# Causal self-attention on f16 high and low parts instead of f32, with the query and key rows turned tile by tile inside the attention's block

## The reference

```
x = x + cross_attention(layernorm(x), context)   # 16 heads, fake-quantised to 8 bits
x = x + self_attention(layernorm(x))             # the part that is changed
x = x + ffn(layernorm(x))                        # FP4 weights, 2816 hidden, RMS norm of the result

# self_attention, B=4 batches, S=128 tokens, H=16 heads of D=64:
q, k, v = x@Wq + bq, x@Wk + bk, x@Wv + bv        # rope on q and k
scores = einsum('bshd,bthd->bhst', q, k) / sqrt(64), -inf above the diagonal
out = einsum('bhst,bthd->bshd', softmax(scores), v) @ Wo + bo
```

## Time and profile before

| | us |
|---|---|
| median of the runs | 2849.79 |
| the profiled execution | 2849.09 |
| its span, first to last instruction | 2847.3 |
| TensorE busy in the span | 2580.7 |
| VectorE busy | 1833.1 |
| ScalarE busy | 1041.4 |
| GpSimd busy | 554.3 |
| mean granted TensorE clock | 0.969 of full speed |

### The profile page before, as it was taken

How to read it: one execution, slowest core, us unless ns; L and a number is a source line. 1 busy time by engine, 2 the same in 40 slices (tenths; PEclk the granted TensorE clock), 3 DMA queues, 4 the chain that set the end, 5 groups by cost and what they waited for, 6 DMA issues and landing times. The chain is left out here.

```text
span 2847.3 us, 42128 instructions
## 1 busy us (share of the span) xinstructions
PE 2580.7 (91%) x16680; PEld 1315.8 (46%) x16680; DVE 1833.1 (64%) x2736; ACT 1041.4 (37%) x929; POOL 554.3 (19%) x206
## 2 busy tenths in 40 slices
PE   6999999999999999999967777777777999999998
PEld 3444444444444444444434444444444448544443
DVE  5855555555555555555488999999983434667673
ACT  3111111111111111111278999999992215311100
POOL 0500000000000000000055664654631280100100
PEclk9999999999999999999999999999998995899999
DMA  6233443443344344334377889788865214000000
GB/s 244 59 101 99 118 103 87 112 110 89 95 125 109 75 110 119 93 91 118 93 183 185 187 199 207 182 197 206 187 134 209 89 60 76 1 16 1 15 4 30
DMA packets 557198, 321.52 MB, mean 113 GB/s; under 512 B 401953, under 2 KB 533281, under 8 KB 552353
## 3 DMA queue, kind: packets, MB, share of 16 engines
q1 hardware_dynamic: 557088, 319.91, 44.2%
HBM read 149.95 MB, written 69.21 MB: 77 GB/s over the span
## 5 line engine op out<-in xcount | busy, mean ns | idle before, releaser
L502 PE MATMUL kv_acc<-kv_whi,kv_xthi 128*128 128x512 f16 x2048 | 777.4, 380 | 5.3 <-DVE kv_xtlo L558 5.3
L502 PE MATMUL kv_acc<-kv_wlo,kv_xthi 128*128 128x512 f16 x2048 | 777.4, 380 | 0.0
L502 PE MATMUL kv_acc<-kv_whi,kv_xtlo 128*128 128x512 f16 x2048 | 777.2, 379 | 0.0
L957 DVE TENSOR_SCALAR_CACHE_REDUCE at_sc<-at_score 128x1024 f32<-128x1024 f32 x512 | 609.7, 1220 | 26.0 <-PE at_score L838 21.6
L1055 ACT ACTIVATE at_sc<-at_sc,at_bias,at_qs 128x4096 uint16<-128x4096 f32 x128 | 484.8, 3791 | 0.9 <-DVE at_bias L969 0.9
L545 ACT ACTIVATE kv_parts<-kv_key 128x1024 f16<-128x1024 f32 x64 | 67.6, 1057 | 863.5 <-DVE kv_key L583 863.5
L502 PEld LDWEIGHTS kv_acc<-kv_whi,kv_xthi 128*128 128x128 f16 x2048 | 200.6, 98 | 247.9 <-DVE kv_xtlo L558 5.8
L502 PEld LDWEIGHTS kv_acc<-kv_whi,kv_xtlo 128*128 128x128 f16 x2048 | 200.7, 98 | 242.4 <-issue 1.4
L502 PEld LDWEIGHTS kv_acc<-kv_wlo,kv_xthi 128*128 128x128 f16 x2048 | 200.6, 98 | 241.9 <-issue 1.1
L564 DVE SCALAR_TENSOR_TENSOR kv_key<-kv_acc,kv_bias 128x512 f32<-128x512 f32 x128 | 88.5, 691 | 339.7 <-PE kv_acc L502 339.7
L853 PE MATMUL at_turn<-ident,at_sc 128*128 128x128 f16 x2048 | 150.4, 223 | 122.2 <-DVE at_probt L975 91.8
(11 more groups left out here) (203 smaller groups left out, 3125.8 us busy)
## 6 DMA issues: line engine op xcount, KB each, us to landing
kv_rows<-in_ctx SPq DMA_DIRECT2D x64, 512.0 KB, 7.9
keys_turned<-kv_kt SPq DMA_DIRECT2D x32, 1024.0 KB, 5.2
values<-kv_val SPq DMA_DIRECT2D x32, 1024.0 KB, 9.5
at_v_raw<-values SPq DMA_DIRECT2D x16, 2048.0 KB, 8.7
at_kt<-keys_turned SPq DMA_DIRECT2D x32, 512.0 KB, 5.2
x<-keys_turned SPq DMA_DIRECT2D x31, 512.0 KB, 5.1
wq_stage<-in_wkv SPq DMA_DIRECT2D x4, 2048.0 KB, 7.5
x<-in_x SPq DMA_DIRECT2D x2, 2048.0 KB, 8.2
```

The source lines that it names most:

```text
L502: last = nc.tensor.matmul(acc[c][:], a[s][:, k, :], b[:, c, k, :], start=(k == 0 and q == 0), stop=(k == KD - 1 and q == 2))
L957: nc.vector.tensor_scalar(sc[n % 2][:, c * SC:(c + 1) * SC], score[pos % 2][:], 1.0, None, ALU.mult, ALU.max, accum_out=part_max[n % 2][:, ...
```

## The change

- q, k, v and the probabilities are kept as f16 high and low parts, scaled by 16 (q, k, v) and by 1024 (probabilities: ln 1024 is added to the negated maximum by one more small VectorE instruction). Scores and sums are three f16 products in place of one f32 product; four transposes of f32 probabilities become eight of f16.
- The turning block is gone. Its turns are units of one matrix (16 of them: tile, half, q or k), `turn_rows`, four transposes each, three ahead of the loop, one behind `scores(0)` and then one per group up to group 11. ScalarE makes the high part (`high_rows`), VectorE the low part (`low_rows`).
- GpSimd splits the probabilities of each group, between `exps` and `turns`, and before its first group the second half of v in four tiles of three instructions. The first half of v is split at the end of the projection before by ScalarE and VectorE (`values_high`, `values_low`).
- The turned probabilities are copied out by ScalarE in even groups and by VectorE in odd ones, as 16-bit words.
- The bias rows of q, k and v serve as buffers; the feed-forward loads wait until all 16 units are turned.
- Panel 9 is split in the output projection, behind the fourth unit of o, and the products, takes and normalisations go in a new ORDER: (0,0), (1,0), (0,1), (1,1), (2,0), ...
- The wait of `exps` for the reciprocals and the order of TensorE's queue in the loop are as they were.

```diff
@@ attend_causal, sync
             sp.dma_start(*row).then_inc(feed.row_loaded, 16)
+            sp.wait_ge(y_turned, len(units))
             feed.load(sp, 0)
@@ tensor
+            def turn_rows(n):
+                t, h, q = units[n]
+                if n >= 2:
+                    pe.wait_ge(lo_ready, n - 1)
+                for k in range(4):
+                    at = (4 * h + k) * P
+                    last = nc.tensor.transpose(y_bank[n % 2][:, k, :], (y_q, y_k)[q][:, t, at:at + P], ident32[:])
+                last.then_inc(y_turned, 1)
+
             def scores(g):
...
+                pe.wait_ge(lo_ready, 4 * t + 2 * (c // 2) + 2)
...
+                    for n, (a, b) in enumerate(((0, 0), (0, 1), (1, 0))):
+                        last = nc.tensor.matmul(score[g % 2][:, j, :], q_parts[a][rows, at, tok], k_parts[b][rows, at, tok],
+                                                start=(n == 0), stop=(n == 2))
             def turns(g):
-                pe.wait_ge(exps_done, HG * (g + 1))
+                pe.wait_ge(p_split, g + 1)
                 if g >= 2:
-                    pe.wait_ge(p_out, g - 1)
-                for j in range(HG):
-                    last = nc.tensor.transpose(turn[g % 2][:, j, :], s[g % 2][:, j, :], ident32[:])
+                    pe.wait_ge(p_out[g % 2], g // 2)
+                for n in range(2 * HG):
+                    last = nc.tensor.transpose(turn[g % 2][:, n, :], p_parts[g % 2][:, n, :], ident16[:])
                 last.then_inc(p_turned, 1)
...
+            for n in range(3):
+                turn_rows(n)
             scores(0)
+            turn_rows(3)
             for g in range(G):
                 if g + 1 < G:
                     scores(g + 1)
+                if g + 4 < len(units):
+                    turn_rows(g + 4)
                 turns(g)
                 if g >= 1:
                     sums(g - 1)
@@ vector
             for g in range(G):
-                if g == G // 2:
-                    panels.low(dve, split)
                 if g + 1 < G:
                     masks(g + 1)
+                if g + 4 < len(units):
+                    low_rows(g + 4)
+                if g % 2:
+                    turned_out(g)
                 if g >= 1:
                     outputs(g - 1)
@@ scalar
             for g in range(G):
+                if g + 4 < len(units):
+                    high_rows(g + 4)
                 if g + 1 < G:
                     exps(g + 1)
-                turned_out(g)
-                if g == G // 4:
-                    panels.high(act, split)
+                if g % 2 == 0:
+                    turned_out(g)
+        @block.gpsimd
+        def _(pool):
+            def split_values(t):
+                half = slice(HALF, D)
+                nc.gpsimd.tensor_scalar(y_v[:, t, half], y_v[:, t, half], PART, None, ALU.mult).then_inc(v_step, 1)
+                pool.wait_ge(v_step, 2 * t + 1)
+                nc.gpsimd.tensor_copy(v_parts[0][:, t, half], y_v[:, t, half]).then_inc(v_step, 1)
+                pool.wait_ge(v_step, 2 * t + 2)
+                nc.gpsimd.tensor_tensor(v_parts[1][:, t, half], y_v[:, t, half], v_parts[0][:, t, half], ALU.subtract)\
+                    .then_inc(v_split, 1)
+            def split_probabilities(g):
+                pool.wait_ge(exps_done, HG * (g + 1))
+                if g >= 2:
+                    pool.wait_ge(p_turned, g - 1)
+                hi, lo = p_parts[g % 2][:, 0:HG, :], p_parts[g % 2][:, HG:2 * HG, :]
+                nc.gpsimd.tensor_copy(hi, s[g % 2]).then_inc(p_hi_ready, 1)
+                pool.wait_ge(p_hi_ready, g + 1)
+                nc.gpsimd.tensor_tensor(lo, s[g % 2], hi, ALU.subtract).then_inc(p_split, 1)
+            for t in range(T):
+                split_values(t)
+            for g in range(G):
+                split_probabilities(g)
@@ project_and_feed_forward, vector
             for n in range(len(units)):
                 low_o(n)
+                if n == 3:
+                    panels.low(dve, first + 1)
             make(0)
             dve.wait_ge(row_added, 1)
-            for t in range(T):
-                take_x(t, 0)
-                take_x(t, 1)
-                normalise(t)
-                if t:
+            for t, n in ORDER:
+                take_x(t, n)
+                if n == 1:
+                    normalise(t)
+                if n == 1 and t:
                     low_x(2 * t - 2)
                     low_x(2 * t - 1)
```

More of the change, by code:

```diff
@@ L262, in project @@
 def project(chip, tag, panels, first, count, split_first, split_after, rows, addend, out, added=None, beside=None,
-            stats=None):
+            stats=None, after=None):
     nc = chip.nc
@@ L288, in _ @@
                 panels.high(act, m)
+            if after is not None:
+                after[1](act)
         @block.vector
@@ L308, in _ @@
                     panels.low(dve, m)
+                if after is not None and n == after[0]:
+                    after[2](dve)
             dve.wait_ge(panels.taken, T * (first + count))
@@ L1100, in rotate, with attend_causal @@
     return n + 4 * T
-def attend_causal(chip, y_q, y_k, y_v, mask, o, ident32, q_t, panels, split, feed, row):
+def attend_causal(chip, y_q, y_k, y_v, mask, o, ident32, ident16, q_parts, v_parts, spare, feed, row):
     nc = chip.nc
-    turned, q_out, k_out = chip.sem("ca_turned"), chip.sem("ca_q_out"), chip.sem("ca_k_out")
-    scored, masked, maxed = chip.sem("ca_scored"), chip.sem("ca_masked"), chip.sem("ca_maxed")
-    exps_done, p_turned, p_out = chip.sem("ca_exp"), chip.sem("ca_p_turned"), chip.sem("ca_p_out")
+    y_turned, hi_ready, lo_ready = (chip.sem(f"ca_{n}") for n in ("turned", "hi", "lo"))
+    v_step, v_split, p_hi_ready, p_split = (chip.sem(f"ca_{n}") for n in ("v_steps", "v_split", "p_hi", "p_split"))
+    scored, masked = chip.sem("ca_scored"), chip.sem("ca_masked")
+    max_found, maxed = chip.sem("ca_max_found"), chip.sem("ca_maxed")
+    exps_done, p_turned = chip.sem("ca_exp"), chip.sem("ca_p_turned")
+    p_out = [chip.sem("ca_p_out_scalar"), chip.sem("ca_p_out_vector")]
     summed, inv_ready, o_ready = chip.sem("ca_summed"), chip.sem("ca_inv"), chip.sem("ca_o")
     HG = 4
+    PART, LN_PROB = X_SCALE, float(np.log(1024.0))
     groups = [(t, c) for t in range(T) for c in range(HEADS // HG)]
     G = len(groups)
+    units = [(t, h, q) for t in range(T) for h in range(2) for q in range(2)]
     def head_of(c, j):
@@ L1123, in attend_causal, with part @@
         inv = [chip.sb(ctx, f"ca_inv{j}", [P, HG], F32) for j in range(2)]
[L1124 to L1155 removed]
+        y_bank = [chip.ps(ctx, f"ca_y{n}", [P, 4, P], F32) for n in range(2)]
         score = [chip.ps(ctx, f"ca_score{n}", [P, HG, P], F32) for n in range(2)]
[L1158 removed]
+        turn = [chip.ps(ctx, f"ca_turn{n}", [P, 2 * HG, P], F16) for n in range(2)]
         outp = [chip.ps(ctx, f"ca_outp{n}", [P, HG, P], F32) for n in range(2)]
         block = ctx.enter_context(nc.Block())
+        def part(n, e):
+            t, h, q = units[n]
+            return parts[q][e][:, 4 * h:4 * h + 4, t * P:(t + 1) * P]
         @block.sync
@@ L1245, in _, with high_rows @@
         def _(act):
+            def high_rows(n):
+                act.wait_ge(y_turned, n + 1)
+                nc.scalar.activation(part(n, 0), y_bank[n % 2][:], ACT.Copy, scale=PART).then_inc(hi_ready, 1)
             def exps(g):
@@ L1385, in project_and_feed_forward, with done @@
     units = [(t, h) for t in range(T) for h in range(2)]
+    ORDER = [(0, 0), (1, 0), (0, 1), (1, 1)] + [(t, n) for t in range(2, T) for n in range(2)]
+    def done(t, n):
+        return ORDER.index((t, n)) + 1
     with ExitStack() as ctx:
@@ L1449, in products @@
             def products(t, n):
+                pe.wait_ge(panels.lo_ready, first + n + 1)
                 pe.wait_ge(o_lo_ready, 2 * t + 2)
                 if t >= 2:
-                    pe.wait_ge(wo_taken, 2 * (t - 2) + n + 1)
+                    pe.wait_ge(wo_taken, done(t - 2, n))
                 w_hi, w_lo = panels.parts[first + n]
@@ L1474, in _ @@
                 turn_o(n)
-            pe.wait_ge(panels.lo_ready, first + 2)
-            for t in range(T):
-                for n in range(2):
-                    products(t, n)
-                if t:
+            for t, n in ORDER:
+                products(t, n)
+                if n == 1 and t:
                     turn_x(2 * t - 2)
@@ L1641, in _ @@
                 high_o(n)
+                if n == 3:
+                    panels.high(act, first + 1)
             act.wait_ge(feed.raw_loaded, 16 * GROUPS)
```

119 lines of the change are left out of this document (64 added, 55 removed).

## The result

| | before | after |
|---|---|---|
| median of the runs, us | 2849.53 | 2869.55 |
| spread of the runs | 2849.25 to 2851.23 | 2868.89 to 2870.11 |
| the profiled execution, and its span | 2849.09, 2847.3 | 2869.78, 2868.0 |
| busy: TensorE, VectorE | 2580.7, 1833.1 | 2564.4, 1867.8 |
| busy: ScalarE, GpSimd | 1041.4, 554.3 | 1046.8, 596.7 |

The ratio is 1.0069, with a 95% interval of 1.0051 to 1.0086: the change makes the kernel 20 us slower. 2866.1 was forecast, with 2853 to 2877 as range.

The account below looks back on a forecast made before the run. It took a serial chain through ScalarE, TensorE and VectorE, closed by the reciprocal, to bound the attention loop, with GpSimd put into it. +9.2 (attention) and +7.1 (projection) gave +16.3 us: 2866.1 us, range 2853 to 2877.

Parts of the forecast that it names:

- The chain that the prediction rests on: Attention loop: exponentials, GpSimd's split, turns, sums, reciprocal, next exponentials follow serially; anything between exponentials and turns is paid in full.
- The loop: Attention groups: 5.69 us each against 4.73, +0.96; sums give back 1.10, turns cost 0.10 more, GpSimd 1.96.
- The start: Before the loop: GpSimd's value splits take 11.4 us; exponentials of group 2 at about 2364.1, against 2365.37 before.
- the scaling of a value tile on GpSimd: In `split_values` at the start: 0.80 us for each of four tiles, taken between 0.61 and 1.15.
- The end of the loop: Last exponentials to the next stage's first transpose: 7.56 us against 7.3; the stage begins 9.2 us later.
- The projection: Output projection: normalised rows at 30.7, TensorE idle 4.4 us, clock dip 2.7; +7.1 us, bounds 4.4 and 8.5.
- The moved feed-forward loads: Loads moved behind the last row turn, about 2417: all there by about 2451, costing nothing, with 5 us of cover.
- The hidden value steps: VectorE behind panel 8: four steps of about 0.7 us cost nothing under 4.49 us idle; without cover 2.8.
- The tiny addition in `masks`: VectorE in the attention loop: held by a GpSimd split at most 1.15 us, staying inside the slack.
- B: Rival, chance 0.14: f16 keeps the clock up at 2.4 GHz, 5.0 us a group; +4.4, so 2854 us.
- D: Rival, chance 0.10: clock up as in B and GpSimd's copy costs 0.24; 4.6 us a group, 2845 us.
- C: Rival, chance 0.12: GpSimd's one-input steps cost as much as the subtraction; +28.5, so 2878 us.

Follow-up runs that it names:

- filler: Kernel after plus eight unread f16 products of 256 columns in each group, between the turned rows and the turns of the probabilities: 2864.9 us, ratio 1.0054.
- c1: Kernel after with a third buffer of row totals, panel 9 made in group 0 of the attention and the projection's old ORDER: 2839.6 us, ratio 0.9965.
- late filler: Kernel after with third buffer, value splits behind groups 1, 5 and 9, and eight unread f16 products in each of groups 12 to 15: 2845.2 us.

## Why the prediction was right, and where it wasn't

The forecast's sum was +16.3 us and the profiled execution shows +20.7. Of the 4.4 between them, 1.8 lies ahead of the changed code and isn't the change's, 1.7 is the first turning, 1.5 the attention, and -0.6 the projection with the rest. Part of the closeness is luck: in the attention the start's +3.3 and the loop's -1.7 cancel in part. The chain that the prediction rests on is shown by the runs; by steps:

- **The loop.** Right in every link: 5.69 forecast, 5.59 measured, turns released by GpSimd and exponentials by the reciprocal. GpSimd's copy took 0.61 and the subtraction 1.15, as taken. The one more subtraction shows that all of GpSimd's work there is paid, the third buffer that the chain is closed by the reciprocal. Over 13 groups this was 1.7 us less than forecast, 0.4 of it in the one group at the higher clock.
- **The start.** Mis-sized: exponentials of group 2 came 21.4 us after the first turning, not 18.1. The term is the scaling of a value tile on GpSimd, taken as 0.80 with bounds 0.61 to 1.15; it measured 1.49, above my upper bound. I had bounded it by a two-input subtraction that writes f16. A nearer row stood in the trace of the kernel before: GpSimd's two-input product of 128x512 that writes f32 (line 1087) took 1.50 us where nothing held it (2312.76). Four scalings at 0.69 more are 2.8 of the 3.3; the turns of group 1 came 2.9 us later than forecast, and 0.3 lies behind them. By the Trainium skill (GPSIMD Engine Reference, Engine selection) a one-input operation is near line rate; the copy agrees with it, 0.61, and the scaling, 1.49 for as many columns, doesn't, so the measurement decides. That the value work bounds the start is shown by moving it.
- **The end of the loop.** 7.56 forecast, 7.47 measured.
- **The projection.** +7.1 forecast, +7.65 measured, +6.5 with the rest. Panel 9's low part took 5.63 instead of 4.42: GpSimd's 8.87 us addition ran until 2459.47, 1.35 us into it; the rows came at 31.2 us of the stage (30.7 forecast), TensorE idled 5.03 (4.4), and the dip to 0.50 came as foreseen. With the panel and the ORDER back, all of it was gone. The moved feed-forward loads cost nothing, as forecast: neither ScalarE's scaling nor `make(0)` waits for them.
- **The hidden value steps.** Wrong: costed at nothing under 4.49 us of cover, they cost 1.7. I took their 0.7 from the takes. The take at 2339.56 ran beside GpSimd's rotation too and wasn't slowed, but its first operand is in PSUM, while a value step has both in SBUF; the value steps took 2.58 each. The kernel before had an instruction of their kind in the same stretch, which I didn't weigh (5.98 us, 4.42 in the earlier trace rows):
```profile
2327.73 5.98 DVE L257 SCALAR_TENSOR_TENSOR wt_ring<-wt_stage,wt_ring 128x4096 f16<-128x4096 f32 x1 [3.02 <-ACT wt_ring L252]
2329.51 13.33 POOL L1098 TENSOR_TENSOR space<-space,rope_swapped 128x1024 f32<-128x1024 f32 x4
```
- **The tiny addition in `masks`.** Held for 1.01 us by the split (0.17 without), inside the slack, as the prediction said of the shared port. By the rule cited there (the Trainium skill, Advanced Engine Details and Errata, VectorE Performance Modes, Mode Summary) each side can block the other, and the trace agrees for this addition. The panel back in the loop shows the other side, GpSimd's copy held for 3.45; whether VectorE's panel instruction runs in one of the modes of that rule, no run shows.
- **The rivals.** B's condition, the clock at 1.00, didn't hold beyond the first group, but its price did: 5.0 a group forecast, 5.03 with filler. D's copy of 0.24 didn't come. C's 1.15 didn't come for the copy; for the scaling more than that did, which put a part of C's loss into the start.
- **What the prediction left unsaid.** That the kernel before had TensorE's own f32 work 0.08 us behind its chain, so that the f32 form had no further to go and the f16 form did.

## What to carry to other kernels

A faster product in a loop that is a closed chain buys only its own links, and whatever is put between two links is paid in full; look first at the wait that closes the chain, since here a third buffer of 128x4 totals was worth 26 us and brought the same change from 20 us above the kernel before to 6 below (the same buffer alone, without the change, reaches 3 to 4 below). Then ask what the shorter period does to work that was hidden under the longer one: here two edits that gained 26.5 and 5.8 us alone gained 23.7 together, because a helper engine's 3.4 us no longer fitted. Take a duration from an instruction whose operands lie in the same memories and whose neighbour engine is as busy: the same shape took 0.69 with an operand in PSUM and 2.58 without, both beside GpSimd's rotation.

## What the runs showed of the hardware

- VectorE's 128x512 step with two operands in SBUF took 2.58 us beside GpSimd's two-input instructions of 128x1024 and 0.62 without them; GpSimd's four took 14.68 instead of 13.35. With the first operand in PSUM it took 0.69 beside them.
- In these rows one of the two engines waits for the other's instruction, whichever began first. VectorE's 128x4096 step took 4.42 where it began first, and GpSimd's instruction behind it 5.72 instead of 1.50 (2307.07 in the kernel before) or 3.45 instead of 0.61 (panel back). Where GpSimd's had begun, VectorE's took 5.28 (c1), 5.63 (after) and 5.98 (before): 0.86, 1.21 and 1.56 more, with 1.00, 1.35 and 1.70 of GpSimd's instruction still to run.
- GpSimd's scaling of 128x512 f32 took 1.49 us, its copy of the same size to f16 0.61, its subtraction to f16 1.15, its product to f32 1.50.
- The granted clock: 0.50 with TensorE 5.00 of 5 us busy on f32 products and turns (before with the third buffer), but 1.00 in 2345 to 2355 of the kernel before, with 4.03 and 3.75 of 5 us busy on f32 turnings alone; 1.00 with 2.4 to 3.7 of 5 us busy on f16 and a few f32 turnings (third buffer). In the f16 loop it fell where the row turnings ended, with the filler of the longer period too (2421), but not with the late filler at the shorter one, nor from DMA traffic of 133 to 138 GB/s beside it.
